# Rows kept split with four tags, transposed in 16 bits, and scattered as they are, in a kernel of attention and routed experts

## The reference

```
xn = layernorm(x)                                   # over 256 features, no affine part
q, k, v = xn @ Wq, xn @ Wk, xn @ Wv                 # 16 heads, 4 key/value heads, 128 wide
q, k = rope(q) * xscale, rope(k) / xscale           # rotation by halves, position scale
s = softmax(causal(q k^T / sqrt(128))) v, @ Wo
scores = softmax(xn @ gate_w^T)                     # 16 experts
combine = the 2 largest scores of each token
y = sum over chosen experts e: combine[e] * (swiglu(xn @ w_gate_up[e]) @ w_down[e])   # 176 wide
y = y + swiglu(xn @ shared_gate_up) @ shared_down   # 352 wide
out = x + s * silu(y)
```

## Time and profile before

| | us |
|---|---|
| median of 3 runs | 711.84 (711.3 to 714.89) |
| the profiled execution, its own time | 712.51 |
| its span, from the first to the last instruction | 710.3 |
| up to the value projection of round 0 | 38.95 |
| rounds 0 to 14 | 487.27 |
| from the value projection of round 15 to the end | 184.1 |

### The profile page before, as it was taken

How to read it: one execution, slowest core, us unless ns; L and a number is a source line. 1 busy time by engine, 2 the same in 40 slices (tenths; PEclk the granted TensorE clock), 3 DMA queues, 4 the chain that set the end, 5 groups by cost and what they waited for, 6 DMA issues and landing times.

```text
span 710.3 us, 16035 instructions
## 1 busy us (share of the span) xinstructions
PE 646.2 (91%) x4916; PEld 455.9 (64%) x4981; DVE 576.3 (81%) x1682; ACT 442.5 (62%) x1203; POOL 536.8 (76%) x585
## 2 busy tenths in 40 slices
PE   3668999999999989999999999999998999999982
PEld 1245667676666656666676666676766777777750
DVE  6987999999999998998999999998985454333378
ACT  3576766676565756576666766676777765555541
POOL 4576878779787979899999889899898973555500
PEclk9999999999999999999999999999999999999996
DMA  8582000004100000000000000000043625676773
GB/s 300 188 281 71 2 1 3 1 1 109 47 1 1 8 8 24 23 7 22 15 15 15 15 15 22 22 15 17 1 65 105 199 64 107 149 144 148 229 267 103
DMA packets 64260, 50.28 MB, mean 71 GB/s; under 512 B 34704, under 2 KB 57584, under 8 KB 64208
## 3 DMA queue, kind: packets, MB, share of 16 engines
q1 hardware_dynamic: 60144, 39.19, 19.8%
q0 software_dynamic: 3792, 10.39, 4.9%
q10 hardware_dynamic: 272, 0.02, 0.0%
HBM read 24.73 MB, written 18.69 MB: 61 GB/s over the span
## 4 chain that ended last, share of the span: by engine, by line
POOL 26%; PE 25%; DVE 23%; issue 14%; ACT 6%; DMA 4%; SPq 0%; POOLq 0%; DVEq 0%; ACTq 0%
POOL arena L555 11%; PE bank L1592 8%; POOL arena L542 6%; PE bank L1622 5%; POOL arena L549 4%; DVE arena L1126 4%; ACT arena L778 4%; DVE arena L1101 3%; DVE arena L1100 3%; PE bank L1436 2%; POOL compare L584 2%; POOL xs_dram L588 2%; PE bank L1465 2%; PE bank L1449 2%; DVE arena L1096 2%
## 5 line engine op out<-in xcount | busy, mean ns | idle before, releaser
L555 POOL TENSOR_TENSOR arena<-arena,rinv 128x128 f32<-128x128 f32 (+3 forms) x256 | 176.3, 718 | 51.2 <-DVE rinv L1120 50.8
L778 ACT ACTIVATE arena<-bank,nmax 128x512 f32<-128x512 f32 (+3 forms) x256 | 132.7, 534 | 53.7 <-DVE nmax L1114 53.7
L1114 DVE CUSTOM_DVE_ANT_0 bank<-bank,mask_b 128x512 f32<-128x512 f32 (+3 forms) x256 | 118.0, 516 | 7.0 <-issue 7.0
L1405 PE MATMUL bank<-xnT_hi,arena 128*128 128x512 f16 (+1 forms) x320 | 110.3, 386 | 14.0 <-DVE arena L1101 7.7
L786 ACT CAST arena<-bank 128x512 f16<-128x512 f32 (+1 forms) x192 | 94.1, 526 | 43.8 <-PE bank L1449 43.0
L1436 PE MATMUL bank<-arena 128*128 128x384 f16 (+7 forms) x736 | 113.4, 296 | 3.2 <-POOL arena L549 1.3
L1465 PE MATMUL bank<-arena 128*128 128x512 bf16 (+2 forms) x765 | 115.9, 301 | 0.2
L1126 DVE TENSOR_TENSOR arena<-bank,arena 128x512 bf16<-128x512 f32 (+1 forms) x192 | 108.8, 594 | 4.2 <-ACT arena L786 3.2
L1449 PE MATMUL bank<-ident_f,arena 128*128 128x128 f32 x640 | 93.1, 276 | 13.4 <-DVE arena L1126 8.3
L542 POOL TENSOR_TENSOR arena<-arena 128x512 f32<-128x512 f32 x77 | 98.7, 1281 | 2.9 <-DVE arena L1101 2.9
L549 POOL TENSOR_TENSOR arena<-arena 128x512 bf16<-128x512 f32 x80 | 92.4, 1161 | 4.7 <-ACT arena L766 4.7
(11 more groups left out here) (145 smaller groups left out, 1162.7 us busy)
## 6 DMA issues: line engine op xcount, KB each, us to landing
stage<-w_gate_up SPq DMA_DIRECT2D x16, 352.0 KB
xs_dram<-s_sb SPq DMA_DIRECT2D x3, 1548.0 KB, 12.4
arena<-ys_dram SPq DMA_DIRECT2D x8, 512.0 KB, 7.9
stage<-w_down SPq DMA_DIRECT2D x16, 176.0 KB
stage<-wq SPq DMA_DIRECT2D x4, 512.0 KB, 8.7
stage<-wo SPq DMA_DIRECT2D x4, 512.0 KB, 7.4
stage<-x SPq DMA_DIRECT2D x1, 2048.0 KB, 11.0
out<-s_sb SPq DMA_DIRECT2D x8, 256.0 KB, 2.2
```

The source lines that it names most:

```text
L555: ins = pool.tensor_tensor(pr, pr, rinv[:, par, qt:qt + 1].to_broadcast([P, (qt + 1) * P]), ALU.mult)
L778: ins = act.activation(probs[par][:, P_AT[qt]:P_AT[qt] + n], score_bank[u][:, col:col + n], ACT.Exp, scale=-1.0, bias=nmax[:, par, qt:qt + ...
L1114: ins = dve.tensor_tensor_reduce(score_bank[u][:, col:col + n], score_bank[u][:, col:col + n], mask_b[:, S - n:S], -1.0, 3e38, ALU.add, AL ...
L1405: ins = pe.matmul(ps[:], w[a][:, c * chunk:c * chunk + DH], tokens[m][:, c * TOK:c * TOK + S], start=(c == 0 and n == 0), stop=(c == KC - ...
```

## The change

- **x and its normalised form** live in `s_sb` instead of the arena and a buffer of their own. A new buffer `row_sb` holds for each token the high half, the low half and four tags (both weights, the token's destination, and one more than its second slot), 260 words of 4 bytes. ACT writes the high halves of a whole sequence by one cast (`split_hi`), POOL the low halves by one subtraction (`split_lo`), and POOL then clears that quarter of `s_sb` (`clear_sum`).
- **Transposes.** The x items are transposed from the two halves, each in its 16-bit type (eight transposes an item); ACT copies both out (`x_item_in`), and DVE only frees the bank by a one-element memset (`free_x`), which stands ahead of the row maxima or of the rotation. The items move from round 0 to rounds 2, 3 and 4, two each.
- **Statistics and roots** of later sequences move to DVE in round 0, the root to POOL in round 1 by a power and a refinement (`refine_roots`), normalising to ACT in rounds 1 to 3.
- **The router's** groups of logits move to rounds 1, 3 and 4 (two), the routing steps two rounds later. `tile_experts` leaves DVE: POOL compares, ACT counts.
- **The scatter** reads rows straight from `row_sb` and slots from `slot_u`. It runs in rounds 8 to 13: two tiles in round 8, three a round in 9 to 12, two in 13. POOL's loop over rounds is written out.
- **Reading the tags back**: since a row carries the tags of both choices, POOL works out in the last round which of them holds (`read_tags`, nine small operations).
- **The fill** comes from one row (`fill_rows`), and starts before the last two weight chunks are loaded.
- **The start**: rope tables and two weight chunks are loaded ahead of the later sequences, k is projected before q0 and waits for one chunk only, and the fourth weight chunk's low half is POOL's.

```diff
-DX = D + 2
+TAGS = 4
+DX = D + TAGS
...
+ITEMS_X2 = ["q0", "v", "g1", "q1", "o0", "x20", "k", "o1", "x21", "q2", "o2", "q3", "o3"]
+ITEMS_X3 = ["q0", "v", "g2", "q1", "o0", "x30", "k", "o1", "x31", "q2", "o2", "q3", "o3", "g3"]
...
+X_BATCH = {2: 1, 3: 2, 4: 3}
+WEIGHTS_AT = {(0, 1): 4, (0, 3): 5, (1, 1): 6, (1, 3): 7, (2, 3): 8, (3, 3): 9}
+WEIGHTS_HI_AT = {(0, 0): 4, (0, 1): 5, (0, 3): 6, (1, 0): 7, (1, 1): 8, (3, 0): 9}
...
+LOGITS_AT = {(1, 0): 0, (3, 0): 1, (4, 0): 2, (4, 3): 3}
...
+    def scattered(self, j):
+        if self.early == SCATTER_FROM:
+            return {2: [(0, 0), (0, 1)], 3: [(1, 0), (1, 1)]}.get(j, [])
+        if self.kind != "loop" or self.early is not None:
+            return []
+        if self.i == LATE - 1:
+            return {1: [(NT - 2, 0), (NT - 2, 1)], 3: [(NT - 1, 0), (NT - 1, 1)]}.get(j, [])
+        t = self.i * 3 - (3 * LOOP_FROM - 2)
+        return [[(t, 0)], [(t, 1), (t + 1, 0)], [(t + 1, 1)], [(t + 2, 0), (t + 2, 1)]][j]
...
+            for n in range(N_CHUNKS - 2, N_CHUNKS):
+                load_weights(n)
...
-            for n in range(W_FIRST - 1):
+            pool.memset(power[:], -0.5).then_inc(mask_zero, 1)
+            pool.wait_ge(xn_first, QT)
+            for n in range(W_EARLY):
...
-            def rows_low(t):
-                token = xn[:, bass.ds(t * D, D)].rearrange("p (o d) -> p o d", o=1).to_broadcast([P, TOP_K, D])
-                pool.tensor_tensor(rows_lo, token, rows_hi, ALU.subtract).then_inc(rows_split, 1)
-
-            def scatter(halves=range(TOP_K)):
-                for n in halves:
-                    pool.indirect_dma_start(xs_dram, bass.IndirectOffsetOnAxis(slot_now[:, n:n + 1], 0),
-                                            rows_out[:, n, :], None).then_inc(scattered, 16)
+            def split_lo(b):
+                hi, lo = row_halves(token_tiles(b))
+                pool.wait_ge(rows_hi, b + 1)
+                pool.tensor_tensor(lo, xn_t[:, token_tiles(b), :], hi, ALU.subtract).then_inc(rows_lo, 1)
+
+            def clear_sum(b):
+                pool.wait_ge(rows_lo, b + 1)
+                pool.memset(s_sb[:, b * QT * D:(b + 1) * QT * D], 0.0).then_inc(rows_zero, 1)
+
+            def refine_roots():
+                v, r, inv = var[:, LATER], root[:, LATER], rstd[:, LATER]
+                pool.wait_ge(mask_zero, 2)
+                pool.wait_ge(var_ready, 2)
+                pool.tensor_tensor(inv, v, power[:, LATER], ALU.pow).then_inc(rooted, 1)
+                pool.wait_ge(rooted, 2)
+                pool.tensor_tensor(r, inv, inv, ALU.mult).then_inc(newton, 1)
+                pool.wait_ge(newton, 1)
+                pool.tensor_tensor(r, r, v, ALU.mult).then_inc(newton, 1)
+                pool.wait_ge(newton, 2)
+                pool.tensor_scalar(r, r, -0.5, 1.5, ALU.mult, ALU.add).then_inc(newton, 1)
+                pool.wait_ge(newton, 3)
+                pool.tensor_tensor(inv, inv, r, ALU.mult).then_inc(newton, 1)
+                pool.wait_ge(newton, 4)
+                pool.tensor_tensor(shift[:, LATER], mv[:, LATER, 0], inv, ALU.mult).then_inc(newton, 1)
+                pool.wait_ge(newton, 5)
+                pool.tensor_scalar(shift[:, LATER], shift[:, LATER], -1.0, None, ALU.mult).then_inc(scaled, 1)
...
+            def scatter(t, n):
+                pool.indirect_dma_start(xs_dram, bass.IndirectOffsetOnAxis(slot_u[:, bass.ds(t * TOP_K + n, 1)], 0),
+                                        row_sb[:, bass.ds(t * DX, DX)], None).then_inc(scattered, 16)
...
+            def passed_tiles():
+                pool.wait_ge(tiles_known, 1)
+                pool.tensor_scalar(passed[:], tiles_to[:], digit[:, E_GROUPS:E_GROUPS + 1], None, ALU.is_le).then_inc(passed_known, 1)
+
+            def read_tags():
+                pool.wait_ge(meta_in, 16)
+                pool.tensor_scalar(padding, meta[:, :, 3], 0.0, None, ALU.is_lt)
+                pool.tensor_tensor(tile_w, meta[:, :, 1], meta[:, :, 0], ALU.subtract)
+                pool.tensor_tensor(second, meta[:, :, 3], own_slot, ALU.subtract).then_inc(meta_read, 1)
+                pool.wait_ge(meta_read, 1)
+                pool.tensor_tensor(padding, padding, own_slot, ALU.mult)
+                pool.tensor_scalar(second, second, 0.0, None, ALU.is_equal).then_inc(meta_read, 1)
+                pool.wait_ge(meta_read, 2)
+                pool.tensor_tensor(tile_w, tile_w, second, ALU.mult)
+                pool.tensor_tensor(second, second, padding, ALU.add).then_inc(meta_read, 1)
+                pool.wait_ge(meta_read, 3)
+                pool.tensor_tensor(tile_w, tile_w, meta[:, :, 0], ALU.add)
+                pool.tensor_tensor(second, second, meta[:, :, 2], ALU.add).then_inc(meta_read, 1)
...
+                if rd.first and j == 2:
+                    split_lo(0)
+                if rd.early == 1 and j == 0:
+                    clear_sum(0)
+                if rd.early == 1 and j == 2:
+                    refine_roots()
+                if rd.early in X_BATCH and j == 1:
+                    split_lo(X_BATCH[rd.early])
+                if rd.early in X_BATCH and j == 2:
+                    clear_sum(X_BATCH[rd.early])
...
+                if rd.last and j == 2:
+                    read_tags()
+                for t, n in rd.scattered(j):
+                    scatter(t, n)
...
+            def x_item_in(rd, c):
+                b = X_BATCH[rd.early]
+                name = f"x{b}{c}"
+                at = c * TOK + b * S
+                ps = misc_bank[rd.bank(name)][:]
                 act.wait_ge(misc_ps, rd.item(name))
-                xnT_hi_part(int(name[1]), int(name[2]), misc_bank[rd.bank(name)][:])
-
-            root_of(0)
+                act.copy(xnT[0][:, at:at + S], ps.bitcast(F16)[:, 0:S])
+                act.copy(xnT[1][:, at:at + S], ps.bitcast(BF16)[:, S:2 * S]).then_inc(xnT_in, 1)
...
+                    if rd.first and j == 2:
+                        split_hi(0)
+                    if rd.early == 1 and j == 2:
+                        normalise(1, 0)
+                    if rd.early == 2 and j == 0:
+                        split_hi(1)
+                    if rd.early in X_BATCH and j > 0:
+                        x_item_in(rd, j - 1)
+                    if rd.early in (2, 3) and j > 0:
+                        normalise(rd.early, j - 1)
+                    if rd.early == SCATTER_FROM and j == 0:
+                        slots_in()
+                    if rd.early == SCATTER_FROM and j == 2:
+                        count_passed()
...
+            def later_roots():
+                dve.wait_ge(aggregated, 2 * QT)
+                dve.tensor_scalar(var[:, LATER], mv[:, LATER, 1], EPS, None, ALU.add).then_inc(var_ready, 1)
...
+            def free_x(rd, c):
+                if rd.early in X_BATCH:
+                    dve.wait_ge(xnT_in, KC * (X_BATCH[rd.early] - 1) + c + 1)
+                    dve.memset(x_seen[:], 0.0).then_inc(misc_free, 1)
...
+            def transpose_x_item(rd, c):
+                b = X_BATCH[rd.early]
+                name = f"x{b}{c}"
+                ps = misc_bank[rd.bank(name)][:]
+                pe.wait_ge(rows_lo, b + 1)
+                pe.wait_ge(misc_free, rd.item(name) - 2)
+                for half, out in enumerate((ps.bitcast(F16), ps.bitcast(BF16))):
+                    for q in range(QT):
+                        ins = pe.transpose(out[:, half * S + q * P:half * S + (q + 1) * P],
+                                           row_halves(b * QT + q)[half][:, c * P:(c + 1) * P], (ident_h, ident_b)[half][:])
+                ins.then_inc(misc_ps, 1)
```

407 lines of the change are left out of this document (191 added, 216 removed).

## The result

The kernel after takes 717.84 us (median of 6 runs, 716.2 to 720.03), the kernel before beside it 711.77 us (6 runs). The ratio of the two is put at 1.007, with a 95% interval of 1.0054 to 1.0087 (the two medians alone give 1.0085, inside it). The change makes the kernel 5 to 6 us slower where 704 us and "faster" were forecast. The profiled execution of after took 719.88 us against 712.51 of before.

A forecast was written before the change was run, and what follows sets the result against it. No single engine bounds it, but a round cannot go much below PE's 30.6 us, so the excess can be won. −5.0 − 3.0 − 3.6 + 10.4 − 8.2 + 1.0 = −8.4 from 712.51 gives 704 us, range 695 to 710.

The forecast's parts named there:

- A, the start: Before the first value projection: four things leave DVE's chain, −5.0 us, bounds 3 and 7.
- D, rounds 2 to 4: Two x items land in each round and delay the outputs: 104.5 instead of 94.14 us, +10.4, bounds +3 and +16.
- part C: Round 1: four router groups become one, refine_roots' power taken as hidden; 32.0 instead of 35.60 us, −3.6.
- about 1 us of it is absorbed: Rounds 2 and 3: of the 2.7 us by which L800 comes later, ACT's wait takes up about 1, 1.7 remains.
- B, round 0: Six x items leave, DVE gets twelve statistics and sets the pace: 35.5 instead of 38.52 us, −3.0.
- E, rounds 5 to 13: Rounds 5 to 8 at 31.5 us each, rounds 9 to 13 at 30.85: −8.2, bounds −4 and −10.
- 29.7, under PE's 30.6: Rounds 9 to 13: POOL's work with six scatters and gaps comes to 29.7 us a round, below PE's 30.6.
- F, the end: Last round: read_tags' nine small POOL operations ahead of the last head's division cost +1.0 us, bounds 0 and 3.
- Rival 3: Rounds 2 to 4: each x item costs its whole chain and bank wait, 4.0 us, 24 in all; 718 us, chance 0.10.
- Rival 1: Rounds 2 to 4: x items mostly hidden in DVE and ACT idle time, only +3 us there; 697 us, chance 0.20.
- rival 2: One gain missed: POOL still sets rounds 9 to 13 (+4) or the start gains less (+3); 707 to 708 us, chance 0.15.
- Rival 4: Round 0's new DVE operation and the start's float32 sums stall behind POOL, 3.4 us a stall; 707 us, chance 0.08.

The follow-up runs named there:

- experiment 9: Kernel after, with only ScalarE's two normalisations in rounds 2 and 3 moved behind the cast of the outputs: 715.66 us, ratio 1.0004 to the kernel before.
- experiment 1: Kernel after, with outputs cast before the x item and normalisations in rounds 2 to 4, first free_x behind the row maxima: 708.84 us, ratio 0.994 to before.
- experiment 2: Kernel after, with split_hi(0) one step earlier in round 0 and weight chunk 5's high part a step later: 716.83 us, ratio 1.0053 to before.
- experiment 3: Kernel after, with round 0's twelve statistics and their aggregates behind the q0 rotations and row maxima: 716.83 us, ratio 1.0049 to before.
- experiment 6: Kernel before, with only the 16-column comparison of round 6 moved from VectorE to GpSimd: 712.83 us, ratio 0.9967 to before.
- experiment 10: Kernel after with five changes of order, plus round 8's scatters one and three ahead of its last two divisions, not two and two: 704.7 us, ratio 0.9851 to before.
- experiment 5: Kernel after, with scatters two, one and three ahead of the last three divisions in rounds 9 to 12: 721.36 us, ratio 1.0066 to before.
- experiment 11: Kernel after with five changes of order, plus read_tags moved behind the last division of the last round: 703.68 us, ratio 0.9839 to before.

## Why the prediction was wrong

The place of the trouble was read rightly: "rounds 2 to 4 the longest after it, with DVE waiting for ACT's L800 there and PE waiting for a bank at project_out(2)". Four terms were mis-sized, all in one direction; they make 15 of the 16 us between −8.4 and +7.8.

**A, the start, was right.** −4.8 against −5.0. The sum that took 2.10 us takes 0.69, 0.69 and 0.92 now.

**D, rounds 2 to 4, is the first step that failed**: +17.0 instead of +10.4. The experiments divide the 17.0. With round 3 at a full clock (36.74) the three take 109.5, so 1.6 is round 3's clock in this execution. Moving the normalisations takes them to 105.58 (experiment 9): 3.9. Moving the casts and the first `free_x` too takes them to 100.57 (experiment 1): 5.0. The last 6.4 over the 94.14 of before is nearly all TensorE's own: its busy time is 98.13 in experiment 1 (92.14 in the earlier trace rows), thus 6.0 more, for six items and three groups of router logits. Here lies one mistake. In part C I booked 3.6 us for the three groups that leave round 1, and in part D I counted the x items on top of the old lengths of rounds 2 and 3; group g1, which lands in round 3, was not added, and for the two in round 4 there was a word but hardly a figure. Round 4 missed most, by 2.6 us (36.6 for 34.0). The price of a group is TensorE's (33.29 − 30.43)/4 = 0.7 us, so by estimate three make about 2 of the 6.6 us that part D missed. The second mistake weighs no less: "about 1 us of it is absorbed". Round 2 has no group and ran at a full clock, and it took 36.1 us for 35.0. The waits of 2.57 us after a chain of 0.6 + 1.1 + 1.05 show that almost nothing was absorbed: the cast of the outputs started 1.95 us behind the item's first cast, twice a round, and experiment 1 wins 3.6 of these 3.9 us in round 2. ScalarE's idle time lies ahead of the item (1.64 us, waiting for TensorE) and behind the cast of the outputs (the 1.48 us of the earlier trace rows), and none of it between the two. The transposes of an item were sized well (0.38 + 0.39 us, overlapping, for 0.6), though TensorE's busy time rose by 0.8 us an item in round 2 (32.05 in experiment 1, 30.43 before).

**B, round 0, failed on waits I had not put into the sum.** I compared the busy times of the engines (VectorE 33.66 for my 32.4) and did not ask for `split_lo(0)` what the text asks for every other step: who waits behind it. On GpSimd it stands ahead of a division and its input comes from the end of ScalarE's step; TensorE waited 3.85 us there, of which experiment 2 takes 3.1 away. The statistics stood ahead of the rotation of q0; of TensorE's 2.77 us there they made 1.3 (experiment 3). With both repaired round 0 is 34.75 to 34.79 in three executions and 35.60 in one, where 35.5 was forecast. The gain was there, and the order kept it from being collected.

**C, round 1.** 33.69 for 32.0. I took the power function to be hidden although my own bound was 0.2 to 2 us. It takes 2.3 us for 12 columns, over the bound, and stands ahead of a division. Moved, the round takes 32.35.

**E, rounds 5 to 13.** −4.1 for −8.2. Round 6 took 32.54 for 31.5: it carries the routing step of old round 4, which had shown 32.27, and I wrote 31.5 for all four. Round 8 took 33.34 for 31.5: experiment 6 shows that the comparison of 3.41 us was worth 2.5 of the 4 I gave it, and experiment 10 finds 0.6 more in the scatters of that round. What the other 2 us over 30.7 are stays open; in round 8 GpSimd waits 2.7 us for VectorE ahead of the second division, and this was not tried. Rounds 9 to 13 took 156.36 for 154.2; experiment 5 wins 1.0 of these 2.1 by placing the scatters. GpSimd's 139.57 us in 156.36 are no full engine, so "29.7, under PE's 30.6" was no proof that GpSimd sets nothing.

**F, the end, was right as far as it can be seen.** The +1.5 of the whole stretch says little: it took 184.1 and 187.6 us in two executions of before's code there, 184.9 to 188.2 in kernels with after's. But the transposes behind the last division stand 16.97 us behind the last value projection in before (543.19) and 18.09 in after (550.62), so `read_tags` costs 1.1 us there, for +1.0, and experiment 11 takes them away again.

**The rivals.** Rival 3 gave 718 us and a chance of 0.10. Its time is the measured one, its sum is not: it let the other parts be collected in full (−18.8), while they gave −9.2, and it put 24 us on rounds 2 to 4, which took 17. Rival 1 fell, since almost nothing of the items was hidden. Of rival 2, rounds 9 to 13 came about by half (2.1 us of its 4), and the start did not. Rival 4 did not come about in after: `later_roots` took 0.70 us.

```profile
62.19 1.26 POOL L569 TENSOR_TENSOR arena<-arena 128x512 f32<-128x512 f32 x1
...
62.79 0.70 DVE L1082 TENSOR_SCALAR var<-mv 128x12 f32<-128x12 f32 x1
```

It started beside a GpSimd operation and ended, at 63.49, just behind that one's end at 63.45; in experiment 2 it ended at 62.48, behind one that ended at 62.45. By the Trainium skill (page "SBUF — State Buffer", section "Who interferes with whom") a `tensor_scalar` inside SBUF can contend with GpSimd, and the one that issues second is blocked for the whole instruction of the other; both traces agree. The 3.41 us of the earlier trace rows were more: they began at 248.50 and ended behind the last of three GpSimd instructions in a row, of which only the last is in the earlier trace rows.

## What to carry to other kernels

On engines that run in order, an added operation is priced by what stands behind it: look for the first consumer that another engine waits for, and put casts, statistics and splits behind it, not ahead. Idle time absorbs an added step only if it lies between that step and the consumer. And when work moves between stages, book it twice: as a gain where it leaves, at the same time as a cost where it lands. A repair tried alone may show less than it is worth, because a later wait can grow by part of what it won (experiment 3); try the repairs of one chain together before one is dropped. And where a long stretch wanders by more than the effect, measure to a landmark close behind the change, as in experiment 11.
